# Six columns to a batch, own and shared slots in 22 groups of nodes: a graph layer's segment sums on one core

## The reference

```python
in_agg = jax.ops.segment_sum(edge_feat, receivers, num_segments=N_NODES)
out_agg = jax.ops.segment_sum(edge_feat, senders, num_segments=N_NODES)
to_updater = jnp.concatenate([in_agg, out_agg, node_feat], axis=1)
h = jax.nn.relu(to_updater @ W1 + b1)
x = _layernorm(x + h @ W2 + b2)
```

## Time and profile before

| | |
|---|---|
| median of 3 runs | 1434.71 us (1432.44 to 1435.06) |
| the profiled execution | 1431.8 us |
| its span | 1430.0 us, mean granted clock of PE 0.984 |
| PE busy | 1345.7 us (94%) |
| DVE busy | 1350.9 us (94%) |
| ACT busy | 1009.2 us (71%) |
| POOL busy | 1154.9 us (81%) |
| DMA | 255.41 MB, mean 179 GB/s |

### The profile page before, as it was taken

One profiled execution on the slowest core, in us unless ns is written; L12 is line 12 of the kernel. 1 busy time (PEld: TensorE's weight loads), 2 busy tenths in 40 slices (PEclk: granted clock), 3 DMA queues, 4 the chain that ended last, 5 costly groups with the idle time before them and its releaser, 6 DMA issues.

```text
span 1430.0 us, 63740 instructions
## 1 busy us (share of the span) xinstructions
PE 1345.7 (94%) x23675; PEld 1055.1 (74%) x23675; DVE 1350.9 (94%) x3463; ACT 1009.2 (71%) x2185; POOL 1154.9 (81%) x663
## 2 busy tenths in 40 slices
PE   3559999999999999999999899999999999999896
PEld 2349999999999999999999566566666666566543
DVE  6989999999999999999999999999999999998586
ACT  6528888878888888888778666766776667676443
POOL 3888888888888888888888888888888888888633
PEclk9969999999999999999999999999999999999998
DMA  9327777787777777778888777777767777767541
GB/s 300 46 16 191 191 190 190 191 190 193 196 196 196 194 193 193 196 197 219 218 216 219 186 188 196 185 183 186 181 171 186 187 181 208 166 155 181 97 134 43
DMA packets 216557, 255.41 MB, mean 179 GB/s; under 512 B 99251, under 2 KB 179220, under 8 KB 216214
## 3 DMA queue, kind: packets, MB, share of 16 engines
q1 hardware_dynamic: 123880, 223.88, 49.1%
q0 software_dynamic: 92384, 28.77, 22.4%
q10 hardware_dynamic: 144, 0.67, 0.2%
HBM read 143.18 MB, written 110.08 MB: 177 GB/s over the span
## 4 chain that ended last, share of the span: by engine, by line
PE 51%; DMA 17%; POOL 15%; issue 10%; DVE 6%; ACT 0%; DVEq 0%; POOLq 0%; SPq 0%; ACTq 0%
PE psum L1580 21%; PE psum L1603 19%; DMA out_tables<-payload,target 16%; POOL out_tables L711 15%; PE psum L1557 3%; PE psum L1564 2%; PE psum L1643 1%; PE psum L1776 1%; PE psum L1641 1%; PE psum L1767 1%; PE psum L1788 1%; DMA rows_i<-in_dst 1%; DVE from_group L1072 1%; DVE same L1260 1%; DVE in_group L1109 1%
## 5 line engine op out<-in xcount | busy, mean ns | idle before, releaser
L711 POOL DMA_INDIRECT out_tables<-payload,target x628 | 1121.5, 1786 | 209.7 <-issue 186.3
L1580 PE MATMUL psum<-parts,to_slot 128*128 128x194 bf16 x6552 | 587.2, 248 | 0.2 <-ACT slots_out L806 0.2
L1580 PEld LDWEIGHTS psum<-parts,to_slot 128*128 128x128 bf16 x6552 | 553.7, 98 | 16.3 <-issue 0.4
L1603 PE MATMUL psum<-to_node,slots_in 64*64 64x448 bf16 x9828 | 480.8, 351 | 4.8 <-DVE to_node L1233 4.0
L1603 PEld LDWEIGHTS psum<-to_node,slots_in 64*64 64x64 bf16 x9828 | 283.7, 107 | 180.0 <-issue 5.6
L806 ACT ACTIVATE slots_out<-psum 128x388 bf16<-128x388 f32 (+1 forms) x936 | 366.4, 472 | 55.3 <-PE psum L1580 47.2
L1194 DVE TENSOR_SCALAR to_slot<-iota_h,slot 128x896 bf16<-128x896 f16 x936 | 381.9, 460 | 0.1
L1233 DVE TENSOR_SCALAR to_node<-iota_h,slot_rel 128x448 bf16<-128x448 f16 x819 | 268.6, 346 | 0.8 <-PE psum L1603 0.5
L1233 DVE TENSOR_SCALAR to_node<-iota_rows,slot_rel 128x448 bf16<-128x448 f16 x546 | 236.7, 434 | 0.0
L867 ACT ACTIVATE to_node<-apart 128x448 bf16<-128x448 bf16 x273 | 149.0, 573 | 67.2 <-PE psum L1603 66.5
L830 ACT ACTIVATE payload<-psum 128x256 f32<-128x256 f32 x157 | 60.2, 383 | 180.3 <-PE psum L1643 176.3
(11 more groups left out here) (127 smaller groups left out, 771.6 us busy)
## 6 DMA issues: line engine op xcount, KB each, us to landing
slot_tiles<-slots_out SPq DMA_DIRECT2D x78, 1018.5 KB
feat<-in_edge_attr SPq DMA_DIRECT2D x195, 256.0 KB
slots_in<-slot_tiles SPq DMA_DIRECT2D x40, 970.0 KB
slots_in<-slot_tiles SPq DMA_DIRECT2D x40, 921.5 KB
out_tables<-payload,target POOLq DMA_INDIRECT x628
out_tables<-zeros POOLq DMA_DIRECT2D x4, 1600.0 KB
feat<-out_tables SPq DMA_DIRECT2D x48, 128.0 KB, 2.2
slots_in<-slot_tiles SPq DMA_DIRECT2D x14, 242.5 KB
```

The costliest lines, as they stand in the source:

```text
L711: e.indirect_dma_start(out_tab, at, payload[b][:, t, :], None, element_offset=k * TABLE_ROWS * D, compute_op=ALU.add).then_inc(s_tab[k], 16)
L1580: last = e.matmul(ps_share[r % BANKS][:, o:o + SLOT_W], to_slot[m][:, k, g * P:(g + 1) * P], parts[b][:, SHARE_FROM + MINI * m + k, 1:], s ...
L1603: return e.matmul(ps_groups[g % 2][h][cols, 0:HOT], slots_in[p % RING][rows, j - PART_FROM[p], D * k:D * (k + 1)], to_node[rows, node_buf( ...
```

## The change

The sharing columns of a chunk stay 12, in two batches of six in place of three of four. The nodes form 22 groups of 286, so a batch has 11 tiles. The 64 slots of a group in a batch are no longer open to all columns: each column has 8 of its own (its *home*), and 16 are shared by what the homes don't hold. A tile of home slots therefore needs products from the columns only whose homes lie in it: 31 products a batch, by rounds 3, 3, 4, 3, 12 and 6. The one-hot of a column has 640 elements (two of twelve have 768). In the slot table all homes of column 0 come first, then those of column 1, and so on, and the shared slots last. The tiles of a batch thus no longer belong to one pair of groups, and a load gathers 8 rows of each of six columns, and 16 shared rows, for each of two groups: four DMAs for a part.

There are 4 early, 82 sharing and 12 summing chunks. The 11 pairs of groups by 164 batches are 1804 tiles, in 8 parts for each pair. The slot numbers need more: products that count each column's edges in each group, those that give each edge its group, ranks within a column with what earlier columns left over, and bit operations on DVE that turn rank and group into a slot. On PE the spread and the sums by receiver stand behind all rounds; on ACT `split_hi` stands ahead of the payload, and `split_mid` behind six rounds.

```diff
-FIRST = 2
-MINIS = 3
-MINI = 4
+FIRST = 4
+MINIS = 2
+MINI = 6
-GROUP_NODES = 448
+GROUP_NODES = 286
+HOMES = (8,) * MINI
+SHARED = SLOTS - sum(HOMES)
+HOME_AT = [SLOT_GROUPS * sum(HOMES[:k]) for k in range(MINI + 1)]
-HOT_ROW = 64
-SUMS = 18
+HOT_ROW = 26
+SUMS = 12
-LAST_TILES = 150
+LAST_TILES = TILES
-PARTS = 3 * RING
+PARTS = 2 * RING
...
+            slot_rows = slot_tab.rearrange("g p w -> (g p) w")
+            def load_tiles(g, p, a, z):
+                lo = PART_FROM[p]
+                homes = slot_rows[0:HOME_AT[MINI], :].rearrange("(k r) w -> k r w", k=MINI)
+                for h in range(2):
+                    into = slots_in[p % RING][SLOTS * h:SLOTS * (h + 1), a - lo:z - lo, :].rearrange("p t w -> p (t w)")
+                    group = 2 * g + h
+                    e.dma_start(into[0:SLOTS - SHARED, :],
+                                homes[:, HOMES[0] * group:HOMES[0] * (group + 1), a * SLOT_W:z * SLOT_W]).then_inc(s_slot_in[p % RING], 16)
+                    at = HOME_AT[MINI] + SHARED * group
+                    e.dma_start(into[SLOTS - SHARED:, :], slot_rows[at:at + SHARED, a * SLOT_W:z * SLOT_W]
+                                ).then_inc(s_slot_in[p % RING], 16)
             def load_part(g, p):
-                lo, hi = PART_FROM[p:p + 2]
-                e.dma_start(slots_in[p % RING][:, 0:hi - lo, :].rearrange("p t w -> p (t w)"),
-                            slot_tab[bass.ds(g, 1), :, lo * SLOT_W:hi * SLOT_W].rearrange("g p w -> p (g w)")
-                            ).then_inc(s_slot_in[p % RING], 16)
+                load_tiles(g, p, *PART_FROM[p:p + 2])
...
+            def sharing_chunk(c, i, b, mode, s):
+                split_hi(i + b, c + 1, 1 - b)
+                payload_quad(c, b, mode, 0)
+                put_nodes(s + 1, 1 - b)
+                slots(i, s, b, range(0, ROUNDS))
+                split_mid(c + 1, 1 - b)
+                slots(i, s, b, range(ROUNDS, CHUNK_ROUNDS))
...
-                to_slots(s, 1, range(MINI))
-                to_slots(s, 2, (0, 1))
+                to_slots(s, 1, (0, 1, 2))
+                add_window(c, b, ats, 0)
+                split_rest(c + 1, 1 - b)
+                to_slots(s, 1, (3, 4))
                 targets(c, b, c, mode)
...
+                    for k in range(MINI):
+                        for g in range(SLOT_GROUPS):
+                            last = e.matmul(ps_counts[:, k, g, :], in_group[:, k, g, :], ones_bf[:, 0:2], start=True, stop=True)
...
                     for g in range(SLOT_GROUPS):
+                        last = e.matmul(ps_group, ident_bf[:, :], from_group[:, :, g, :], start=(g == 0), stop=(g == SLOT_GROUPS - 1))
...
+                            for j in range(w):
+                                to = ps_ranks[a][:, BATCH_TILES * j:BATCH_TILES * (j + 1)]
+                                last = e.matmul(to, above_bf[:, :], in_group[:, k, g + j, :], start=True, stop=(k == 0))
+                                if k > 0:
+                                    last = e.matmul(to, earlier_bf[0:BATCH_TILES, k, g + j:g + j + 1].to_broadcast([BATCH_TILES, P]),
+                                                    ident_64[0:BATCH_TILES, 0:BATCH_TILES], start=False, stop=True)
...
-                for r in range(HEAD_ROUNDS, CHUNK_ROUNDS - MINIS):
+                for r in range(HEAD_ROUNDS, CHUNK_ROUNDS):
                     slot_round(s, b, r)
                 spread(c + 1, 0, 0)
-                for r in range(CHUNK_ROUNDS - MINIS, CHUNK_ROUNDS):
-                    slot_round(s, b, r)
                 sum_windows(c, b)
```

351 lines of the change are left out of this document (188 added, 163 removed).

## The result

The changed kernel takes 1766.24 us, median of 4 runs (1758.55 to 1771.11), against 1434.83 us before: a ratio of 1.231 (95% interval 1.225 to 1.237), so 23% slower. The forecast was 1555 (1490 to 1650): the direction and the bound of the summing stage were right, the size was not, by 211 us. The profiled execution has a span of 1769.3 us.

What follows compares the result with a forecast made beforehand. PE and DVE, almost without gaps, bounded the kernel before; loads over six engines would bound the changed sums. Sharing from 203 to 899, 12 for the first summing chunk, 554 of loads, 5 and 80 gave 1550, by the median 1555 us (1490 to 1650).

Steps and rivals of the forecast that it cites:

- likeliest case: Summing stage: six DMA engines carry each part's home rows, so the sums wait for loads; 1500 to 1650 us, chance 0.82.
- Start (+103): Before sharing: two more early chunks and longer slot numbering move the first sharing one-hots from 100 to 203 us.
- numbering: Slot numbers before sharing: two batches of 46.5 us each on DVE and PE, starting at 106.5 us.
- tail: Node update behind the last sums: trimmed from 83 to 80 us.
- A part at 6.6 us: Summing loads: 18 rows x 0.31 us per engine plus scatters and features; 84 parts 554 us; 7.9 with the dearer row.
- Sharing at 8.4 us: Sharing loop: a chunk falls from 8.79 to about 8.4 us, between 8.1 and 8.8; 82 chunks take 689 us.
- The sum of DMA time (7.1 of 8.4 us): Sharing loop: DMA work of 5.0, plus 0.34 for the store and 1.7 for four scatters, stays below the period.
- the summed chain: Sharing loop: PE and ACT steps from spread and windows through hi, payload and evictions to the last rounds, 8.1 us plus 0.3.
- Rival C: B with one cost more: GpSimd's four scatters hold sharing at 8.79 (1462 us), or slow PE counting (1480); chance 0.07.
- First loads at 4 us in sharing: End of sharing: the split-off first loads of the slot tiles add 4 us.
- Rival B: Summing loads: transfers reach 16 engines, a part costs 3.5 us and is hidden; 1425 or 1430 us, chance 0.11.
- C as the clock: Slot numbering: PE counts at the slow clock, +50 us, 1480 us; second form of the rival with chance 0.07.

Runs made afterwards that it cites:

- old_six_blocks: Kernel before, each part's load of 128 rows replaced by the changed kernel's four transfers, same bytes: 1644.87 us, ratio 1.110.
- home16: Changed kernel, each part loaded by eight transfers of 16 rows into every eighth partition, same bytes: 1635.28 us, ratio 1.105.
- early_two: long_parts with eight scatter tables, summed in the tail, and 2 early and 14 summing chunks in place of 4 and 12: 1480.14 us, ratio 1.032.
- home16_8tables: home16 with odd sharing chunks scattering into four further tables, which the final sum leaves out: 1614.58 us, ratio 1.089.
- windows_earlier: one_load_8tables_two with the spread and the sums by receiver ahead of PE's last two slot rounds: 1528.7 us, ratio 1.068.
- one_load_8tables_two: one_load with eight scatter tables and with 2 early and 14 summing chunks: 1518.51 us, ratio 1.060.
- one_load: Changed kernel with shared slots as two further columns of 8, so a part is one transfer of 16 by 8 rows: 1618.94 us, ratio 1.131.
- long_parts: home16 with six parts of 27 tiles per pair, not eight of 20, three buffers, slot_rel 16 tiles later: 1540.51 us, ratio 1.075.

## Why the prediction missed

Two steps failed: the part of the sums at 6.6 us, whose row price was too low, and sharing at 8.4 us, which counted GpSimd's issues and left out the wait for a scatter's landing.

- **Direction, likeliest case and its mechanism: right.** The loads by six engines were forecast from the form of the transfer; the packets in flight, old_six_blocks and home16 show it. The Trainium skill (DMA: Bandwidth & Descriptors, section Why a DMA increments its semaphore by 16 and not by 1) gave the same six; the six packets in flight, and parts 8.6 us apart in old_six_blocks where six engines make 8.4, agree with it.
- **Start (+103), numbering, tail: right** within 6 us. The last 2 early chunks cost 51 us of it (early_two).
- **A part at 6.6 us: the term was mis-sized.** "A row of 20.5 tiles is 7954 B: 0.31 us" took the rate of a moment in which all engines stream. The mean in the summing stretch, gave 0.38 and stood in the same sentence. Rows took 0.38 to 0.41 in the changed kernel, so 18 of them 7.1 us in place of 5.6, and a part 7.7 ((666 - 12 - 5) / 84): 84 parts x 1.1 = 92 of the 95 us. A row's price under the load of the stage was the one to take, and "7.9 with the dearer row" should have been the sum's middle.
- **Sharing at 8.4 us: a wait was left out.** "GpSimd four scatters at the early 1.87 = 7.5" counts only the issues. A scatter also waits until the last one on its table has landed, and that landing with 0.73 us must fit into a period. On the slowest table this was 7.1 + 0.73 of 8.8 before, and 8.4 + 0.73 of 8.6 with the new store where nothing waits for it (home16_8tables). The store's 512 further descriptors made the landing longer while the change made the period shorter. The sum of DMA time (7.1 of 8.4 us) said that it fits. It looked only at engine time, not at how long one scatter's packets stand among others, and it had the store too cheap: a descriptor of 776 B took 49 to 54 ns on average, not 42, so the store added 0.8 to 1.2 us and not 0.34. The wait cost 91 of the 130 us (eight stalls of 8.4 are 67 of them).
- **What sets the 8.4 to 8.6 between stalls: the chain is not shown.** The period came out as summed, but four scatters cost 8.5 under this load, not 7.5 (1.81 to 1.84 us each and 0.30 between them), which fills it too, and windows_earlier shortened the summed chain to no effect. So the number may be right by luck. Rival C named GpSimd; its 8.8 was too high, and its sign, scatters back to back, did come, though it was there before as well. Which of the two holds the period is open.
- **First loads at 4 us in sharing: mis-sized.** The last 16 sharing chunks took 10.9 us each, 2.5 above the period: about 39 us. That six engines carry those loads explains a part at most: with loads over all engines and eight tables (one_load_8tables_two) they still take 9.4. The rest is open.
- **Rival B was priced too low.** "With all 16 a part costs 3.5" assumed 0.31 us a row also there. In one_load 8 rows of 0.52 to 0.57 take 4.4, with the 1.0 for scatters and features 5.4, and its stage took 583 us. Even with every load hidden the kernel would need about 1769 - 225 = 1544 us (an estimate, with the 441 us of another chip), 1.08 of the kernel before, because of sharing.
- **C as the clock:** PE's granted clock was 0.82 between 100 and 197 us, and each batch still took 47.6 us. The slow price didn't come.

## What to carry to other kernels

When a change gives a DMA a new form, ask first over how many engines it is dealt and what SP pays to issue it: in the kernel before the same bytes cost 2 us of waits in the form of 128 rows and 128 in that of 6 x 8 rows (old_six_blocks), and eight small transfers cost SP 5.7 us where one cost 0.33 before. For every resource that is used in turn (a table, a buffer) compare the time from issue to landing with the period, not only the busy time of the engine. And check what a chain of waits says against the resource itself: the chain before put 45% on landings that held nothing up, and the chain with eight tables ran through windows whose place made no difference in windows_earlier.

## What was not expected of the hardware

- A row's price depends on the form of its transfer. Packets of 7760 B: 368 ns in the kernel before (one transfer of 128 consecutive rows), 385 when six engines carry them, 416 as eight transfers of 16 rows, 525 as one transfer of 16 x 8 rows. Neither padding the rows nor trebling their distance changed the last number (530, 522). The cause is open.
- SP issued transfers of 16 rows into every eighth partition in 0.59 us at the median and 0.67 on average, those of 48 and of 16 rows in 0.74 and 0.45, one of 16 x 8 rows in 0.54, one of 128 consecutive rows in 0.33. In long_parts, with rows a third longer, the median was 0.59 too.
- A scatter of 128 rows of 256 B takes 3.4 us to land alone. In the sharing loop before the four tables' took 3.8 to 7.1 on average, and in home16_8tables, beside stores of 1408 descriptors, 3.0 to 8.4; in the changed kernel single ones took up to 10.7.
- The stalls come from a small deficit that adds up: for 7 to 12 chunks nothing is lost, and then a whole period at once. A short piece of the trace between two of them looks like a loop at its best pace.
